# Second stage of a two-layer graph network: y turned ahead of q, first products of the next node tile ahead of linear, their scaling ahead of h

## The reference

```python
xj = node_features[col]
m0 = s @ Wm_ss * dist + einsum('eui,ei->eu', v, r_vec) @ Wm_vv + s @ Lm_s
m1 = (s @ Wm_sv)[:, :, None] * r_vec[:, None, :] + (v, Wm_vs) * dist + (v, Lm_v)
agg = segment_sum(concat(m0, m1), row)                   # a0: 64 scalars, a1: 32 vectors
u0 = einsum('nu,nv,uvw->nw', xs, a0, Wu_ss) + einsum('nui,nvi,uvw->nw', xv, a1, Wu_vv) + xs @ Lu_s
u1 = einsum('nu,nvi,uvw->nwi', xs, a1, Wu_sv) + einsum('nui,nv,uvw->nwi', xv, a0, Wu_vs) + (xv, Lu_v)
x = layernorm(x + node_features + concat(u0, u1))
```

## Time and profile before

| | |
|---|---|
| median of the timed runs | 7424.65 us (7392.01 to 7425.52) |
| profiled execution | 7435.46 us, span 7433.7 us |
| mean granted clock of PE | 0.899 |
| PE busy | 5925.0 us, 80% |
| DVE busy | 5508.1 us, 74% |
| ACT busy | 3744.2 us, 50% |
| POOL busy | 5516.6 us, 74% |

### The profile page before, as it was taken

One profiled execution on the slowest core, in us unless ns is written; L12 is line 12 of the kernel. 1 busy time (PEld: TensorE's weight loads), 2 busy tenths in 40 slices (PEclk: granted clock), 3 DMA queues, 4 the chain that ended last, 5 costly groups with the idle time before them and its releaser, 6 DMA issues.

```text
span 7433.7 us, 146089 instructions
## 1 busy us (share of the span) xinstructions
PE 5925.0 (80%) x52495; PEld 4766.6 (64%) x52495; DVE 5508.1 (74%) x7220; ACT 3744.2 (50%) x11578; POOL 5516.6 (74%) x4470
## 2 busy tenths in 40 slices
PE   4666666666666589888888988898849999999998
PEld 3444544544444477776776776777738888888887
DVE  5766666666666587777777777777728888888888
ACT  2322332222322355555555555555527777777776
POOL 3788878877778447777777777777758888888887
PEclk6777777777777799999999999999969999999999
DMA  6877777777776266676677776766632222222222
GB/s 212 241 226 226 230 220 229 227 215 218 223 225 192 101 199 230 225 238 229 223 237 232 232 240 222 240 232 228 210 119 88 93 94 94 94 94 94 93 94 71
DMA packets 681152, 1381.03 MB, mean 186 GB/s; under 512 B 106047, under 2 KB 487661, under 8 KB 654447
## 3 DMA queue, kind: packets, MB, share of 16 engines
q1 hardware_dynamic: 527695, 1090.23, 46.5%
q0 software_dynamic: 152736, 281.45, 11.2%
HBM read 587.20 MB, written 784.08 MB: 184 GB/s over the span
## 4 chain that ended last, share of the span: by engine, by line
PE 50%; issue 14%; DVE 13%; ACT 10%; another core or an unknown queue 6%; POOL 4%; DMA 1%; SPq 1%; DVEq 0%; POOLq 0%; ACTq 0%
PE node_ps L1352 12%; PE prods_ps L1320 5%; PE prods_ps L1301 5%; ACT onehot L1700 3%; PE prods_ps L1304 3%; DVE zs L1040 3%; POOL slots L649 3%; PE node_ps L1368 2%; PE m_ps L1217 2%; PE m_ps L1368 2%; PE s_ps L1217 2%; PE turn_ps L1339 2%; PE s_ps L1199 2%; ACT onehot L1706 2%
## 5 line engine op out<-in xcount | busy, mean ns | idle before, releaser
L649 POOL DMA_INDIRECT slots<-pay,slot_all x3136 | 3290.2, 1049 | 889.6 <-issue 830.1
L1700 ACT ACTIVATE onehot<-node_iota,msgs 128x125 f32<-128x125 f32 x3400 | 1030.0, 397 | 77.0 <-POOLq L711 77.0
L1352 PEld LDWEIGHTS node_ps<-msgs,onehot 128*125 128x125 f32 x6800 | 932.7, 188 | 145.2 <-issue 104.3
L1352 PE MATMUL node_ps<-msgs,onehot 128*125 128x160 f32 x6800 | 981.0, 303 | 42.4 <-ACT onehot L1706 32.7
L1086 DVE TENSOR_REDUCE upd<-work 125x48 f32<-125x3072 f32 x300 | 1003.7, 3346 | 6.9
L1073 DVE TENSOR_TENSOR work<-prods_ps,yv 125x1024 f32<-125x1024 f32 x800 | 930.3, 1214 | 36.5 <-PE prods_ps L1305 23.4
L1199 PE MATMUL s_ps<-ident,picks_sb 128*125 128x128 f32 x1568 | 389.3, 391 | 618.2 <-issue 567.5
L739 POOL TENSOR_TENSOR q<-xt,yv 125x3072 f32<-125x3072 f32 x100 | 547.7, 5477 | 349.2 <-PE turn_ps L1339 331.6
L724 POOL TENSOR_TENSOR q<-xt,yv 125x512 f32<-125x512 f32 x400 | 428.4, 1073 | 438.6 <-PE turn_ps L1339 415.5
L1199 PEld LDWEIGHTS s_ps<-ident,picks_sb 128*125 128x125 f32 x1568 | 314.0, 278 | 665.6 <-issue 640.9
L1217 PE MATMUL m_ps<-win,picks_sb 125*128 125x160 f32 x3136 | 675.4, 344 | 74.1 <-issue 49.4
(11 more groups left out here) (273 smaller groups left out, 14470.7 us busy)
## 6 DMA issues: line engine op xcount, KB each, us to landing
msgs<-slots SPq DMA_DIRECT2D x200, 1428.0 KB, 6.3
slots<-zero SPq DMA_DIRECT2D x183, 1386.0 KB
win<-table SPq DMA_DIRECT2D x784, 160.0 KB
picks<-picks_sb SPq DMA_DIRECT2D x196, 512.0 KB
picks_sb<-picks SPq DMA_DIRECT2D x196, 512.0 KB
table<-tab SPq DMA_DIRECT2D x200, 350.0 KB
slots<-pay,slot_all POOLq DMA_INDIRECT x3136
spill_in<-spill_sums SPq DMA_DIRECT2D x200, 80.0 KB, 6.1
```

What stands on the lines that cost most here:

```text
L649: g.indirect_dma_start(out=slots[layer][:, :], out_offset=bass.IndirectOffsetOnAxis(ap=slot_all[:, j:j + 1], axis=0), in_=pay[q][:, j - UB ...
L1352: te.matmul(node_ps[0:HM, 0:D], onehot[:, j, :], msgs[b][:, j, 0:D], start=(j == 0), stop=False)
L1700: last = ac.activation(onehot[:, j, :], node_iota[:, :], ACT.Square, bias=msgs[b][:, j, LOCAL:LOCAL + 1], scale=-1.0)
```

## The change

In the second stage three things move; nothing is added or removed, and the third stage keeps its order. `turn_y` stands behind the row sums and ahead of both turns of q, on PE, and `turned_y` likewise on ACT. `bilinear(0)` of tile t stands ahead of `linear` of tile t - 1 on PE, and `bilinear(1)` directly behind it and ahead of message (1,1). `scalars(0)` of tile t stands on DVE at the end of step t, ahead of h of tile t - 1; until now it opened step t + 1. The wait of message (1,1) for the copies of y is gone, since `bilinear(0)` waits for them ahead of it.

```diff
@@ vector, node_step @@
-                def scalars(r):
+                def scalars(r, n=n, nb=nb):
...
                 if nodes and layer == 0:
-                    scalars(0)
                     scalars(1)
                     q_first()
...
                     mixed_sum(R0 + 1)
+                if layer == 0 and within(t, 0, NT):
+                    scalars(0, t, b)
                 if nodes:
                     ve.wait_ge(*((s["lin_out"], n + 1) if layer == 0 else (s["lin"], n + 1)))
@@ tensor, node_step @@
                 scalar_sums()
+                turn_y()
                 turn_q(0)
                 message(1, 0)
                 turn_q(1)
-                turn_y()
+                bilinear(0, t, b)
                 linear()
-                bilinear(0, t, b)
-                if edges:
-                    te.wait_ge(s["y_turned_out"], 3 * t + 3)
+                bilinear(1, t, b)
                 message(1, 1)
-                bilinear(1, t, b)
@@ scalar, node_step @@
                 scalars_out()
+                turned_y()
                 turned_q(0)
...
                 turned_q(1)
-                turned_y()
                 paid(1, 0)
```

## The result

The changed kernel took 7512.0 us (median of 4, 7507.1 to 7523.5), the kernel before beside it 7418.0 (7392.0 to 7425.5): a ratio of 1.0127, interval 1.0102 to 1.0151. The forecast was 7355 us in 7295 to 7432; it went the other way. Two repeats on other occasions gave 1.0118 and 1.0153; one, on an occasion when the kernel before took 7098 us, gave 0.9976. The experiments show what goes with the difference.

The account below looks back on a forecast made before the run. Message steps were taken as bound by a chain handing over between PE and ACT, early steps by DVE. 93 steps at 0.75 us save 70 us: 7435.5 profiled becomes 7365.5, or 7355 against timed runs, range 7295 to 7432.

Parts of the forecast that it names:

- Part one: On PE and ACT, y ahead of q: q's turns and copies 0.31 us later, y's 0.46 us of copies hidden.
- room for 0.6: On ACT ahead of the first copy of q: 0.6 us idle, enough to hide y's copies of 0.46 us.
- the slower rival: On ACT, table's copies behind message (1,1) delay table's rows: +0.43 us a step (0.6 if q's copies stall), 7465; chance 0.13.
- Part two: On PE, first products fill linear's 0.66 us wait; linear and message (1,1) 0.43 us later, work behind 0.66 earlier.
- Part three: On DVE, first scaling ahead of h: h 0.43 us later, third products on PE start 1.3 us earlier.
- The unknown: In message steps, first products and table's rows land some 2.3 us after their records; three ways this could go.
- the third way: Lateness belongs to the place in the step: message (1,1) lands 0.43 us later, some 0.4 to 0.7 still saved.
- first way: Lateness goes with the first products and holds linear: message (1,1) 0.4 us later, 0.7 us a step saved behind it.
- The other lateness: 2.3 us between the last record of the table's rows on PE and ACT's copy of them.
- the credit for the third products: On PE, third products, 1.3 us earlier, leave the path to the table's rows; said against the slower rival.
- The seven early steps: First seven node steps, before any second-layer message, DVE-bound (98.24 of 100 us): no gain, length unchanged.
- the forecast of 0.75 a step: Net saving in each of 93 message steps, 0.75 us, taken near the first way; chance 0.54 for 0.4 to 1.1.

Follow-up runs that it names:

- e1: Kernel before with only y turned ahead of q on PE and copied ahead of q on ACT: 7393 us, 1.0183 of before.
- e6: Changed kernel run again unchanged, in the third comparison: 7520 us, 1.0118 of the kernel before.
- e14: Changed kernel run again unchanged, in the fifth comparison: 7529 us, 1.0153 of the kernel before.
- e5: Kernel before run again unchanged with a profile, in the third comparison: ratio 1.0006.
- e17: Kernel before run again unchanged with a profile, in the fifth comparison: ratio 1.0001.
- e16: Changed kernel with the fourth products ahead of the table's rows, fifth comparison: 7453 us, 1.0062 of before.
- e4: Changed kernel with the fourth products ahead of the table's rows, second comparison: 7233 us, 0.9956 of before.
- e3: Changed kernel with message (1,1) again ahead of the second products, directly behind linear: 7312 us, 1.0075 of before.
- e18: Changed kernel run again unchanged, in the sixth comparison, where no completion is late: 7082 us, 0.9976 of before.
- e15: Changed kernel with the table's two copies ahead of the selections on ACT, completions late: 7545 us, 1.0178 of before.
- e8: Changed kernel with twelve identity transposes on PE between the third products and the wait for tv_t: 7538 us, 1.0148 of before.
- e10: Kernel before with the fourth products ahead of the table's rows, no completion late: 7127 us, 1.0046 of before.
- second and third comparison: Two of six side-by-side timings on one chip each; the kernel before took 7268 us and 7430 us in them.
- e19: Changed kernel with one more DMA in each of 92 message steps, writing 0.95 MB of zeros: 7135 us, 1.0048 of before.
- Copies-first: Changed kernel with the table's two copies ahead of the selections on ACT, run twice: 0.9931 and 1.0178 of before.
- rows-later: Changed kernel with the fourth products ahead of the table's rows, run twice: 0.9956 and 1.0062 of before.

## Why the prediction was wrong

**Part one was right to 0.07.** From the end of the row sums, the second turn of q starts 1.62 us later instead of 1.24 in the middle step, +0.38 where 0.31 was forecast (1.62 in e1, e6 and e14 too, 1.24 in e5 and e17). Of this 0.32 is PE's, since the first turn of q ends at 0.90 instead of 0.58. The copies of y are nearly hidden, though not because ACT has room for 0.6: they end at 4044.06, where the first copy of q starts, and the turn of q was done at 4043.99 (rows of after). That the copies of q are stalled by the full 0.46, as the slower rival had it, did not come. In the mean of all steps it is +0.45 (1.55 to 2.00), because in some of them a turn lands late.

**Part two was right.** The first products fill linear's wait. In the middle step linear starts 3.29 us behind the row sums instead of 2.87 and the records of message (1,1) end at 8.01 instead of 7.59, both +0.42 with 0.43 forecast. Behind the edge sum the table above has 0.77 and 0.74, since the row sums themselves end later in the mean, which no term of the forecast had: 2.86 to 3.11, and +0.28 and +0.26 in the two repeats (e5 to e6, e17 to e14). Their issue stalls grew from 46.2 to 54.9 us; what the rest is stays open.

**Part three was right in what it counted.** The third products start 1.30 us earlier (13.60 to 12.30), as forecast to the tenth.

**The unknown went by the third way.** The first products in their new place land 0.02 us after their records; the second products, behind linear, are late by 2.20, as the first products were (2.26). This lateness belongs to the place behind linear, and message (1,1) is copied 0.62 later (12.40 to 13.02). The forecast's first way, a late first product that holds linear, had nothing to act on: linear's landing is 0.31 late, and was 0.37. The other lateness, that of the table's rows, went away: ACT takes them up 0.44 us behind their records instead of 1.81 in the middle step.

**The step that failed** is the credit for the third products: "Against it: those products, 1.3 us earlier, leave that path." They left it, and the path did not get shorter, because the table's copies stood only 4029.64 - 4029.42 = 0.22 us behind them in the earlier trace rows. So at most 0.22 of the 1.3 could come out; over the stage it was 0.17: from ACT's start on message (1,1) to the table's rows it is 2.29 us in the middle step of before and 2.12 in that of after. The copies, queued behind message (1,1)'s pay and the selections, moved 0.61 the other way (14.21 to 14.82), and the rows start at 15.14 instead of 14.68, +0.46. That is the wait which the slower rival named, with 0.13 of the chances. Of the experiments, e16 covers this wait with work and gets 0.9% back beside e14; e4 and e3 have the lowest ratios of their comparison, with less lateness too; e18 has 0.3 us of it a step and no loss. But to take the wait away is not enough: e15 and e8, in which it is down to 11.8 and 22.7 us, are as slow as after.

**What the rival lacked.** It gave 0.43 us a step, 7465; the step grew by 0.76. It also let the rows' later start reach the table's landing, and that came earlier: ACT's copy starts at 16.93 us instead of 17.84. The larger part of the growth stands behind the start of the rows, as PE's own busy time. Means over the message steps, from the traces:

| before to after | rows start | rows to next edge sum | PE busy in it | PE idle in it | its clock | step |
|---|---|---|---|---|---|---|
| first | 14.87 to 15.07 | 9.19 to 9.67 | 8.14 to 8.98 | 1.05 to 0.69 | 0.99 to 0.90 | 29.21 to 29.97 |
| e5 to e6 | 15.02 to 15.42 | 8.93 to 9.38 | 8.05 to 8.71 | 0.88 to 0.66 | 1.00 to 0.93 | 29.10 to 30.00 |
| e17 to e14 | 14.86 to 15.30 | 8.92 to 9.52 | 8.05 to 8.81 | 0.87 to 0.71 | 1.00 to 0.91 | 28.94 to 29.97 |

The forecast had no term for the clock. In 41 of the 93 steps in after's trace it is between 0.50 and 0.75 over the 4 us from the start of the rows, and in each of these PE had stood idle ahead of them, for 1.8 us in the middle one; in 27 other steps with such a hole of over 1 us it did not fall. So the 69 us of the message steps are PE's busy time (+68 us), and behind the start of the rows alone this grew by 0.84 us a step, 77 us in all. e8 shows that filling the hole brings the clock back; it also shows that this alone does not bring the time back, since pay waits and issue stalls took over.

**The seven early steps** did not stay at their length. They take 154.8 or 154.9 us in the three traces of before, and 169.8, 177.8, 179.8 (e6, e14) and 186.5 (e18) in those of after. The seven steps in before and then in after:

```profile
2540.00:2694.80 154.80, 134.42 (x1404) 109.50 (x1404) 145.31 (x113) 91.37 (x302) 28.93 (x28) 0.97 0.40 132
```

```profile
2521.40:2691.20 169.80, 147.96 (x1403) 121.02 (x1404) 145.76 (x113) 91.66 (x302) 28.93 (x28) 0.89 0.37 120
```

With e18's row above: PE's idle time is 20.4, 21.8 and 21.7 us, its busy time 134.4, 148.0 and 164.8, at clocks of 0.97, 0.89 and 0.80. Busy time times clock stays at 130 to 132 us, so what grew is the time at the lower clock. The forecast called these steps DVE's, with no term for it. In after the first products wait 9.2 us there (6 times, 1.5 at most) for the bank of DVE's last mixed product, which the earlier trace rows put at the beginning of the mixed sum and the forecast took as over. This wait is not shown to be the cause: e18 has the same 9.2 us at a lower clock, and e1, with part one alone and without this wait, took 167.8 us at 0.88. What lowers the clock there stays open.

The whole profiled span grew by 71.7 us (7433.7 to 7505.4): 69.4 in the message steps, 15.0 in the early ones and 5.8 behind them, less 18.6 in the part ahead, whose program is the same.

In e18 the whole is 16 us faster than the kernel before. If before's early steps took 155 us there too (e10, with none late, has 156.5), after lost 32 us in them, and the message steps gave back about 48 us, 0.5 a step: an estimate, as before has no profile in that comparison. So with no late completions the forecast of 0.75 a step had the sign right and was half as much again too large; its 7355 us, for an occasion with late ones, was wrong.

## What to carry to other kernels

When an instruction's last releaser is moved earlier, credit only the gap to the second-latest, and read that gap in the same timeline before anything else; here it was 0.22 us of a claimed 1.3. A copy that other work queues behind (ACT's pay, selections, copies) carries any lateness of its releaser on to all of them. A hole that a change opens on PE ahead of packed work may cost more than itself: here the 4 us of work behind it ran at 0.50 to 0.75 of the clock in 41 steps of 93. And a distance within a step is read step by step, since medians of two places can belong to different steps: that distance was 1.24 us here where the medians had 1.32, and 1.62 where they had 2.21.

## What was not expected of the hardware

Completions of matmuls came 2.2 us late in some comparisons and 0.02 us in others, for the same program, and the kernel before took 7418 or 7094 us with them. The second and third comparison even carry the same chip number (7268 and 7430 us). In a trace with late ones, message (1,1) lands 3.3 to 3.4 us behind the end of linear in the middle step of before, after, e5, e6, e8, e14 and e17, whichever products stand there, and in that step within 0.1 us of the landing of those products, though its records end 0.8 us behind theirs; in e18, with none late, it is 1.84. More DMA did not bring them about (e19). Their cause stays open. The sign of the change goes with them: 1.012 to 1.015 with late completions, 0.998 without, in four comparisons. Copies-first gave 0.993 where none is late and 1.018 where they are, where rows-later gave 1.006 against after's 1.015; rows-later alone was not run on the changed kernel where none is late. No version was shown to beat the kernel before on both kinds of occasion.
